# Three elementwise steps of a cross-attention and feed-forward kernel are issued by GpSimd in place of VectorE

## The chip, the cores and the metric

The program runs on 1 core of one Trainium2 chip. The metric is the device time in microseconds (us) of one execution. The kernel before took 1811.93 us, the median of 3 runs (1809.35 to 1813.45).

A core has engines that run their own instruction streams in order and meet at semaphores: TensorE (PE; its weight loads are PEld), VectorE (DVE), ScalarE (ACT), GpSimd (POOL), and SyncE (SP), which here only waits and issues transfers.

## The reference

All inputs are float32. There are 4 batches, with 1024 rows of `x` and 2048 rows of context each, 512 columns, 16 heads of 32.

```python
x = x + xattn(layernorm(x), ctx, ctx, mask, W_q, W_k, W_v, W_o)
x = x + ffn(layernorm(x), rhs)

# xattn
q, k, v = (Q @ W_q.T), (K @ W_k.T), (V @ W_v.T)          # split into 16 heads of 32
scores = einsum('bhqd,bhkd->bhqk', q, k) / sqrt(32)
e = where(mask, exp(clip(scores, -50, 50)), 0)
attn = e / sum(e, -1)                                    # 1 where the sum is <= 0
out = einsum('bhqk,bhkd->bhqd', attn, v) @ W_o.T

# ffn: int8 product with a scale per row of lhs and per column of rhs
q_lhs = clip(round(lhs / lhs_scale), -127, 127)          # lhs_scale = max|row| / 127
y = (q_lhs @ q_rhs) * lhs_scale * rhs_scale
```

## The kernel before

**Segments.** The work is a list of 21 segments. A segment can hold up to three kinds of work: *a*, the projections K, V and Q of a batch; *b*, the attention of a group of 4 heads (32 steps: 2 halves of 512 queries, each over 16 key tiles of 128); *c*, the row tiles (128 rows each) of the batch before: output projection, layer norm, int8 quantisation, feed-forward, residual, store. The first 4 segments have only *a*. The 12 that follow have *a* and *b*, the last 8 of them *c* too, with 2 row tiles each; they run from about 141 to 1375 us, and this text calls them the shared segments. Then come 4 final segments with *b* and 3 row tiles each, to about 1770 us, and the last 4 row tiles by themselves. The remaining entry of the list holds no attention.

**Slots.** A segment has 32 slots, one for each attention step. The tables `BOTH`, `ENDING` and `ENDING_LAST` say at which slot a piece of *a* or *c* is issued (`("F", 0)` is the feed-forward product of row tile 0). Each engine walks over the slots and issues its share; what it does then waits on semaphores with constant values, so the tables set the order on each engine and not the time.

**Attention of a step.** PE writes the scores of 4 heads into 4 banks, ACT turns them into exponentials (`probs`, L1169), PE multiplies these with V (`wsum`, L943). For the denominators DVE adds the exponentials of steps 0 to 13 of a half into `acc` (L1455, 128 x 2048, both operands in SBUF). `probs` is a ring of 4 steps: ACT may write step s only once DVE has added step s - 4.

**End of a half.** Each half that is done goes through a chain, in the slots of the half that follows (`first` is 0 or 16 there): ACT copies `denoms` and `sums` out; SP spreads the denominators (slot first + 2), DVE inverts them (L1463), SP stores the reciprocals and loads them back, broadcast to all rows, into `denoms` (L724, slot first + 5). Then three steps follow: `sums` times `denoms` (L1471, on DVE, behind slots first + 8 and first + 9), the rounded part cast by ACT into `o_hi` (L1271, at first + 10), and `sums` minus that part (L1474, on DVE, behind first + 12 and first + 13). SP then writes both parts to DRAM (`o_parts`, L731, at slot first + 14). These are what the output projection of the next batch reads.

**Row tile.** PE computes the output projection (`O`), DVE adds the residual and takes the row statistics (L1350 to L1354), POOL raises the variance to the power -0.5 (`rstd`, L1545; in the final segments L547, of 128 x 1 elements each). DVE then normalises (L1388, or L1492 in the final segments), finds the maximum, quantises (L1393, L509); ACT rounds (L1191, L521); PE transposes (`T`) and multiplies (`F`); DVE scales the product (L1438, L514) and adds the residual (L1511; in the final segments `add_rows`, L552). SP stores the rows and loads the rows of the next tile into the same buffer, both after `y_added`.

**POOL** has little else to do. At the start of a segment it reads the flag that says whether clipping can be left out (it can, for these inputs) and then releases all `probs_ready` waits of the segment at once.

## Time and profile before

| | |
|---|---|
| median of 3 runs | 1811.93 us |
| profiled execution | 1813.45 us |
| its span in the trace | 1811.6 us |
| PE busy | 1726.3 us (95%), 10808 matmuls |
| DVE busy | 1382.8 us (76%), 1663 instructions |
| ACT busy | 1299.1 us (72%), 1713 instructions |
| POOL busy | 110.7 us (6%), 76 instructions |
| granted PE clock, mean | 0.983 |
| moved by DMA | 295.94 MB, mean 163 GB/s |

The span is the time from the first to the last instruction in the trace; the execution's own time is 1.85 us longer. Busy time of PE is modelled from pipelined matmuls, so a PE that is busy all the time can still be held up inside a matmul stream. The page's 40 slices of the span show PE at 9 tenths or more in nearly all slices, except the first and some of the last ten:

```profile
PE   7999999999999999999999999999998989898986
DVE  5647777777778878787887878788785888787785
POOL 0000000000001010100101010000100000000001
```

### The profile page before, as it was taken

What the parts mean: (1) busy time and instruction counts of PE and PEld (TensorE: products, weight loads), DVE (VectorE), ACT (ScalarE), POOL (GpSimd) and SP (SyncE); (2) the same over time, 40 slices, a digit from 0 to 9 for tenths busy, and PEclk for the clock granted to TensorE, in tenths of its full rate; (3) what the DMA queues carried; (4) which work ended last, traced back from release to release, by engine and by line L of the source; (5) the groups of instructions that cost most, each with busy time, mean ns of one, the idle gap of its engine ahead of it and who ended that gap; (6) DMA issues with size and microseconds to landing.
All of it is one profiled execution on the core that took longest, in us unless ns stands there. A gap on an engine that the chain in (4) does not pass through costs nothing.

```text
span 1811.6 us, 30523 instructions
## 1 busy us (share of the span) xinstructions
PE 1726.3 (95%) x10808; PEld 1015.2 (56%) x10808; DVE 1382.8 (76%) x1663; ACT 1299.1 (72%) x1713; POOL 110.7 (6%) x76
## 2 busy tenths in 40 slices
PE   7999999999999999999999999999998989898986
PEld 6895655555565565656655565666554343343433
DVE  5647777777778878787887878788785888787785
ACT  4557777778777777777777777777775767666672
POOL 0000000000001010100101010000100000000001
PEclk9999999999999999999999999999999999999997
DMA  7686655556665665567566556757557786768632
GB/s 254 212 245 152 159 143 139 141 140 156 158 172 143 166 163 148 169 154 198 125 159 177 147 168 150 198 127 177 157 151 188 196 188 162 162 163 203 157 94 76
DMA packets 231173, 295.94 MB, mean 163 GB/s; under 512 B 28136, under 2 KB 134632, under 8 KB 230504
## 3 DMA queue, kind: packets, MB, share of 16 engines
q1 hardware_dynamic: 228856, 289.21, 61.1%
q10 hardware_dynamic: 2160, 4.72, 0.9%
q8 instruction: 88, 1.44, 0.4%
q14 instruction: 69, 0.57, 0.1%
HBM read 201.59 MB, written 92.00 MB: 162 GB/s over the span
## 4 chain that ended last, share of the span: by engine, by line
PE 78%; issue 8%; DVE 6%; ACT 4%; DMA 2%; POOL 1%; SPq 1%; POOLq 0%; DVEq 0%; ACTq 0%
PE tile L905 24%; PE wsum L943 22%; PE scores L927 21%; ACT probs L1169 3%; PE tile L975 3%; PE scores L905 3%; DVE acc L1455 2%; PE tile L969 2%; PE scores L1073 1%; POOL kmax L547 1%; PE tile L1036 1%; PE tile L1073 1%; DMA v_parts<-v_stage 1%; PE tile L1013 1%; DMA wq_lo<-o_parts 1%
## 5 line engine op out<-in xcount | busy, mean ns | idle before, releaser
L1169 ACT ACTIVATE probs<-scores 128x1024 f32<-128x1024 f32 x939 | 914.1, 1027 | 232.1 <-PE scores L927 177.8
L1455 DVE TENSOR_TENSOR acc<-acc,probs 128x2048 f32<-128x2048 f32 x384 | 878.8, 2288 | 132.4 <-ACT probs L1169 122.3
L943 PE MATMUL wsum<-probs,v_sb 128*32 128x512 f32 x4096 | 501.9, 608 | 0.0
L927 PE MATMUL scores<-q_stack,k_stack 128*128 128x512 f32 x1536 | 444.5, 410 | 9.4 <-ACT probs L1169 8.9
L927 PEld LDWEIGHTS scores<-q_stack,k_stack 128*128 128x128 f32 x1536 | 265.5, 188 | 222.9 <-ACT probs L1169 111.2
L943 PEld LDWEIGHTS wsum<-probs,v_sb 128*32 128x32 f32 x4096 | 111.6, 110 | 257.1 <-issue 230.9
L1545 POOL TENSOR_TENSOR rstd<-var_eps,minus_half 128x1 f32<-128x1 f32 x48 | 79.6, 1658 | 1255.9 <-DVE var_eps L1354 1255.9
L1073 PE MATMUL scores<-q_stack,k_stack 128*128 128x512 f32 x342 | 109.8, 423 | 23.2 <-ACT probs L1169 23.2
L1406 DVE TENSOR_TENSOR squares<-squares 128x128 bf16<-128x128 bf16 x160 | 35.4, 221 | 122.2 <-ACT squares L1209 122.2
L905 PE MATMUL tile<-ctx_hi,wk_hi 128*128 128x256 f32 x412 | 115.6, 281 | 1.8 <-DVE ctx_lo L1364 1.8
L1169 ACT ACTIVATE probs<-tile 128x1024 f32<-128x1024 f32 x85 | 87.5, 1029 | 38.7 <-PE tile L1073 38.6
L905 PE MATMUL tile<-ctx_hi,wk_lo 128*128 128x256 f32 x412 | 115.2, 280 | 0.0
L905 PE MATMUL tile<-ctx_lo,wk_hi 128*128 128x256 f32 x412 | 115.1, 279 | 0.0
L1455 DVE TENSOR_TENSOR acc<-probs 128x2048 f32<-128x2048 f32 x32 | 73.4, 2293 | 48.3 <-ACT probs L1169 47.1
L1073 PEld LDWEIGHTS scores<-q_stack,k_stack 128*128 128x128 f32 x342 | 57.8, 189 | 86.6 <-ACT probs L1169 48.4
L905 PE MATMUL tile<-wv_lo,ctx_hi 128*128 128x512 f32 x208 | 84.2, 405 | 0.0
L905 PE MATMUL tile<-wv_hi,ctx_hi 128*128 128x512 f32 x208 | 83.9, 403 | 0.0
L905 PE MATMUL tile<-wv_hi,ctx_lo 128*128 128x512 f32 x208 | 82.6, 397 | 0.0
L905 PEld LDWEIGHTS tile<-ctx_hi,wk_hi 128*128 128x128 f32 x412 | 77.4, 188 | 5.8 <-issue 2.6
L905 PEld LDWEIGHTS tile<-ctx_hi,wk_lo 128*128 128x128 f32 x412 | 77.4, 188 | 3.1
L905 PEld LDWEIGHTS tile<-ctx_lo,wk_hi 128*128 128x128 f32 x412 | 77.4, 188 | 0.0
L1206 ACT CAST stage_hi<-tile 128x256 fp32r<-128x256 f32 x144 | 53.8, 374 | 29.6 <-PE tile L905 17.1
(235 smaller groups left out, 2041.9 us busy)
## 6 DMA issues: line engine op xcount, KB each, us to landing
k_stack<-k_parts SPq DMA_DIRECT2D x312, 256.0 KB, 7.1
q_stack<-q_parts SPq DMA_DIRECT2D x124, 256.0 KB, 6.8
v_sb<-v_parts SPq DMA_DIRECT2D x80, 256.0 KB, 6.1
v_parts<-v_stage SPq DMA_DIRECT2D x64, 256.0 KB, 5.1
raw<-ctxT SPq DMA_DIRECT2D x27, 512.0 KB, 6.6
k_parts<-stage_hi SPq DMA_DIRECT2D x96, 128.0 KB, 3.5
k_parts<-stage_lo SPq DMA_DIRECT2D x96, 128.0 KB, 2.0
x_in<-x SPq DMA_DIRECT2D x33, 256.0 KB, 3.8
```

Of the source, the lines that this page charges most:

```text
L547: nc.gpsimd.tensor_tensor(one(f_rstd, n), one(f_var, n), minus_half[:, :], ALU.pow).then_inc(fs["rstd_ready"], 1)
L905: last = nc.tensor.matmul(dst, s(kc), m(kc), start=(n == 0), stop=(n == len(todo) - 1))
L927: last = nc.tensor.matmul(scores[:, h, :], k_stack[:, kt // 4, h, (kt % 4) * P:(kt % 4 + 1) * P], q_stack[:, qb, h, :], start=True, stop=True)
L943: last = nc.tensor.matmul(wsum[DH * h:DH * h + DH, :], v_sb[:, kt, DH * h:DH * h + DH], probs[:, n % RING, h, :], start=(kt == 0), stop=(k ...
L969: last = nc.tensor.matmul(dsum[DH * h:DH * h + DH, :], ones[:, :], acc[:, h, :], start=not opened, stop=False)
L975: last = nc.tensor.matmul(dsum[DH * h:DH * h + DH, :], ones[:, :], probs[:, m % RING, h, :], start=False, stop=(m == n + 1))
L1073: last = nc.tensor.matmul(score_banks(seg, n, pair)[:, h, :], k_stack[:, kt // 4, 2 * pair + h, (kt % 4) * P:(kt % 4 + 1) * P], q_stack[:, ...
L1169: nc.scalar.activation(probs[:, slot % RING, 2 * pair:2 * pair + 2, :], score_banks(seg, slot, pair), ACT.Exp, scale=1.0 / math.sqrt(DH)). ...
L1206: nc.scalar.copy(to, src[:, 0:ROWS]).then_inc(sems["hi_done"], 1)
L1406: nc.vector.tensor_tensor(run if opens else both[:, 0:P], both[:, 0:P], both[:, P:2 * P], ALU.max) \
L1455: nc.vector.tensor_tensor(acc[:, :, :], other, probs[:, slot % RING, :, :], ALU.add).then_inc(sems["add_done"], 1)
L1545: nc.gpsimd.tensor_tensor(rstd[:, u:u + 1], var_eps[:, u:u + 1], minus_half[:, :], ALU.pow).then_inc(sems["rstd_ready"], 1)
```

## The change

Three steps are issued by GpSimd (`nc.gpsimd.tensor_tensor`) where VectorE issued them: the product of `sums` and `denoms`, the subtraction that leaves the low part, and the addition of the residual to the feed-forward product. In the segments with attention the product stands at slot first + 6 of POOL's stream, the subtraction at first + 11, the addition at the slot of its `F` piece (in the final segments at the odd slot of the pair of `F`). SP waits for the low part, and stores both parts, at slot first + 13, one slot earlier than before; within a slot this comes ahead of all else that SP does.

```diff
-        def add_rows(eng, tensor_tensor, n):
-
-            eng.wait_ge(fs["y_scaled"], n + 1)
-            tensor_tensor(f_n(n), f_n(n), f_x1(n), ALU.add).then_inc(fs["y_added"], 1)
+        def add_rows(pool, n):
+
+            pool.wait_ge(fs["y_scaled"], n + 1)
+            nc.gpsimd.tensor_tensor(f_n(n), f_n(n), f_x1(n), ALU.add).then_inc(fs["y_added"], 1)
...
-                    if slot == first + 14:
+                    if slot == first + 13:
                         ct.wait_alone(sp, "attn_split", k)
...
-                def normalise(even):
-
-                    for first, k, on in ((0, 0, seg.prev and seg.b), (KT, 1, seg.b)):
-                        if on and even == first + 8:
-                            ct.wait(dve, "recips_loaded", 16 * k)
-                            ct.wait(dve, "sums_copied", k)
-                            nc.vector.tensor_tensor(sums[:, :], sums[:, :], denoms[:, :], ALU.mult).then_inc(sems["attn_normed"], 1)
-                        if on and even == first + 12:
-                            ct.wait(dve, "attn_hi", k)
-                            nc.vector.tensor_tensor(sums[:, :], sums[:, :], o_hi.bitcast(F32), ALU.subtract).then_inc(sems["attn_split"], 1)
...
-                        n = row_tile(seg, pair, "F")
-                        if n is not None:
-                            add_rows(dve, nc.vector.tensor_tensor, n)
                         invert(even)
-                        normalise(even)
...
-                                    if p[0] == "F" and not soon:
-                                        ct.wait(dve, "y_scaled", p[1] + 1)
-                                        nc.vector.tensor_tensor(normed[:, :], normed[:, :], xr[:, :], ALU.add).then_inc(sems["y_added"], 1)
...
+            def normalise(ct, k):
+
+                ct.wait(pool, "recips_loaded", 16 * k)
+                ct.wait(pool, "sums_copied", k)
+                nc.gpsimd.tensor_tensor(sums[:, :], sums[:, :], denoms[:, :], ALU.mult).then_inc(sems["attn_normed"], 1)
+
+            def normalised_lo(ct, k):
+
+                ct.wait(pool, "attn_hi", k)
+                nc.gpsimd.tensor_tensor(sums[:, :], sums[:, :], o_hi.bitcast(F32), ALU.subtract).then_inc(sems["attn_split"], 1)
...
+                        if p[0] == "F":
+                            ct.wait(pool, "y_scaled", p[1] + 1)
+                            nc.gpsimd.tensor_tensor(normed[:, :], normed[:, :], xr[:, :], ALU.add).then_inc(sems["y_added"], 1)
...
+                        n = row_tile(seg, slot // 2, "F")
+                        if n is not None:
+                            add_rows(pool, n)
+                    for first, k, on in ((0, 0, seg.prev), (KT, 1, seg.b)):
+                        if on and seg.b and slot == first + 6:
+                            normalise(ct, k)
+                        if on and seg.b and slot == first + 11:
+                            normalised_lo(ct, k)
```

On DVE, in a shared segment with row tiles, the stream before is this from the quantisation of the first row tile on:

```order
L1388 TENSOR_SCALAR normed<-xr,mean_var,rstd 128x512
L1389 TENSOR_REDUCE amax<-normed 128x1
L1390 TENSOR_SCALAR row_scale<-amax 128x1
L1391 RECIPROCAL inv_scale<-row_scale 128x1
L1393 TENSOR_SCALAR normed<-normed,inv_scale 128x512
L1455 TENSOR_TENSOR acc<-acc,probs 128x2048
L1406 TENSOR_TENSOR kmax<-squares 128x128
L1410 TENSOR_TENSOR stage_lo<-tile,stage_hi 128x256
L1455 TENSOR_TENSOR acc<-acc,probs 128x2048 x3
L1471 TENSOR_TENSOR sums<-sums,denoms 128x512
```

The product stood behind four accumulations. It and the two other steps are gone from this stream. On POOL the same kind of segment (without clipping) is now this, with lines of the changed kernel (L1537 the power, L1521 the product, L1550 the addition, L1526 the subtraction):

```order
L1537 TENSOR_TENSOR rstd<-var_eps,minus_half 128x1 x2
L1521 TENSOR_TENSOR sums<-sums,denoms 128x512
L1550 TENSOR_TENSOR normed<-normed,xr 128x512
L1526 TENSOR_TENSOR sums<-sums,denoms 128x512
L1537 TENSOR_TENSOR rstd<-var_eps,minus_half 128x1 x2
L1521 TENSOR_TENSOR sums<-sums,denoms 128x512
L1550 TENSOR_TENSOR normed<-normed,xr 128x512
L1526 TENSOR_TENSOR sums<-sums,denoms 128x512
```

Before, POOL had only the four power operations there. The product now stands directly behind the power of the first row tile. On SP, at the end of the last shared segment and the start of the final ones, the stream before is:

```order
L667 DMA k_stack<-k_parts 32x4x512 x4
L697 DMA v_sb<-v_parts 128x512
L868 DMA q_parts<-stage_hi 128x256
L868 DMA q_parts<-stage_lo 128x256
L731 DMA o_parts<-denoms 128x512
L731 DMA o_parts<-sums 128x512
L812 DMA safe_row<-safe 1x16x1
L873 DMA v_parts<-v_stage 128x4x128
L558 DMA xr<-x 128x512
L569 DMA wq_hi<-o_parts 128x4x512
L569 DMA wq_lo<-o_parts 128x4x512
```

and with the change:

```order
L731 DMA o_parts<-denoms 128x512
L731 DMA o_parts<-sums 128x512
L667 DMA k_stack<-k_parts 32x4x512 x4
L697 DMA v_sb<-v_parts 128x512
L868 DMA q_parts<-stage_hi 128x256
L868 DMA q_parts<-stage_lo 128x256
L812 DMA safe_row<-safe 1x16x1
L873 DMA v_parts<-v_stage 128x4x128
L558 DMA xr<-x 128x512
L569 DMA wq_hi<-o_parts 128x4x512
L569 DMA wq_lo<-o_parts 128x4x512
```

The two `o_parts` stores moved ahead of a key load (4 transfers), a value load and two query stores; the loads `wq_hi` and `wq_lo`, which read them, stayed where they were.

## Rows read from the trace of the kernel before

**Rows 1.** Busy time by stretch; columns: us, engine busy (x instructions), granted clock, DMA.

```profile
541.00:961.00 420.00, 419.11 (x2694) 252.02 (x2688) 339.84 (x404) 321.35 (x424) 31.26 (x16) 1.00 0.61 161
...
1370.00:1790.00 420.00, 370.68 (x2093) 169.89 (x2092) 319.42 (x291) 273.25 (x314) 23.88 (x14) 0.96 0.67 166
```

**Rows 2.** Waits from 541 to 1370; waiter <- releaser: total us, times, longest.

```profile
DVE acc L1455 <- ACT probs L1169: 68.4, 79, 3.0
...
PE tile L905 <- DVE ctx_lo L1364: 0.9, 1, 0.9
```

**Rows 3.** Timeline, the first row tile of one segment.

```profile
660.72 0.53 SPq L724 DMA_DIRECT2D denoms<-recip_row  x1
...
663.07 2.57 POOL L1545 TENSOR_TENSOR rstd<-var_eps,minus_half 128x1 f32<-128x1 f32 x1 [1.58 <-DVE var_eps L1354]
...
665.68 0.55 DVE L1375 TENSOR_SCALAR x_in<-x_in,mean_var,rstd 128x512 f32<-128x512 f32 x1 [0.44 <-POOL rstd L1545]
...
666.14 0.54 DVE L1388 TENSOR_SCALAR normed<-xr,mean_var,rstd 128x512 f32<-128x512 f32 x1
...
668.35 0.63 ACT L1191 ACTIVATE q<-normed 128x512 bf16<-128x512 f32 x1 [1.22 <-DVE normed L1393]
...
668.88 1.92 ACT L1169 ACTIVATE probs<-scores 128x1024 f32<-128x1024 f32 x2
...
670.52 1.17 PE L927 MATMUL scores<-q_stack,k_stack 128*128 128x512 f32 x4
```

**Rows 4.** Timeline, first row tile of a final segment.

```profile
1501.36 2.57 POOL L547 TENSOR_TENSOR kmax<-kmax,minus_half 128x1 f32<-128x1 f32 x1 [35.02 <-DVE kmax L502]
...
1503.97 0.55 DVE L1492 TENSOR_SCALAR v_stage<-x_in,kmax 128x512 f32<-128x512 f32 x1 [0.44 <-POOL kmax L547]
...
1505.66 0.49 DVE L509 TENSOR_SCALAR v_stage<-v_stage,kmax 128x512 f32<-128x512 f32 x1
...
1506.18 0.63 ACT L521 ACTIVATE raw<-v_stage 128x512 bf16<-128x512 f32 x1 [2.83 <-DVE v_stage L509]
...
1507.77 0.74 PE L1073 MATMUL tile<-q_stack,k_stack 128*128 128x512 f32 x2 [2.93 <-ACT probs L1169]
```

**Rows 5.** Timeline, from the last shared segment into the final ones.

```profile
1361.91 0.62 ACT L1271 CAST denoms<-sums 128x512 fp32r<-128x512 f32 x1
...
1367.89 0.32 SPq L868 DMA_DIRECT2D q_parts<-stage_lo  x1
...
1372.27 0.38 SPq L731 DMA_DIRECT2D o_parts<-denoms  x1
...
1391.79 0.79 PE L905 MATMUL tile<-wo_hi,wq_hi 128*128 128x512 f32 x1 [6.72 <-DMA wq_lo<-o_parts]
```

**Rows 6.** The chain that ended last, same stretch; columns: start us, us, what.

```profile
1372.69 7.17 DMA o_parts<-sums
...
1381.58 10.17 DMA wq_lo<-o_parts
```

**Rows 7.** Line views, moved operations and power; duration in ns min/median/max.

```profile
L1471 DVE TENSOR_TENSOR sums<-sums,denoms x31: 682/685/689, 217.4 to 1758.6; 128x512 f32<-128x512 f32 x31
...
L1511 DVE TENSOR_TENSOR normed<-normed,xr x16: 683/685/690, 578.7 to 1358.2; 128x512 f32<-128x512 f32 x16
...
L552 POOL TENSOR_TENSOR probs<-probs,acc x4: 1259/1261/1262, 1795.3 to 1808.0; 128x512 f32<-128x512 f32 x4
...
L1545 POOL TENSOR_TENSOR rstd<-var_eps,minus_half x48: 547/2573/2632, 23.2 to 1334.7; 128x1 f32<-128x1 f32 x48
```

**Rows 8.** Timeline, one power operation under an accumulation; columns: start us, us, engine, line.

```profile
704.31 2.29 DVE L1455 TENSOR_TENSOR acc<-acc,probs 128x2048 f32<-128x2048 f32 x1
...
704.44 2.57 POOL L1545 TENSOR_TENSOR rstd<-var_eps,minus_half 128x1 f32<-128x1 f32 x1 [10.73 <-DVE var_eps L1354]
...
706.52 0.22 DVE L1406 TENSOR_TENSOR squares<-squares 128x128 bf16<-128x128 bf16 x1
```

**Rows 9.** Busy time by stretch, 1378 to 1381: the DMA share is the last but one.

```profile
1378.00:1381.00 3.00, 3.00 (x29) 0.94 (x32) 0.16 (x1) 2.18 (x4) 0.00 (x0) 1.00 0.33 106
```

More of the change, by code:

```diff
@@ L658, in last_rows_gpsimd @@
                 if n >= FULL + 2:
-                    add_rows(pool, nc.gpsimd.tensor_tensor, n - 2)
+                    add_rows(pool, n - 2)
         def load_k(eng, j, quarter):
@@ L1518, in body @@
                     invert(even)
-                    normalise(even)
                 assert links == ct.per("dve_chain", seg), links
```

## The prediction

> **What bounds the kernel now.** I read the busy time by stretch first, since a mean over the span mixes stages. In the shared segments PE is the bound: of the 420 us from 541 on it is busy 419.11, at a granted clock of 1.00 (the upper of its two levels, 2.4 GHz), with DVE busy 339.84 and POOL 31.26 [rows 1]. In the final segments it is not: 370.68 of 420 us, at a mean clock of 0.96. Second, the waits. From 541 to 1370 us PE waited once, 0.9 us, for anything; DVE waited 68.4 us in 79 places for exponentials, so it catches up with ACT again and again, and work taken from it turns into more waiting there [rows 2]. Third, the timelines of the two places where PE hangs on ACT and ACT on DVE: the first row tile of a shared segment [rows 3] and that of a final segment [rows 4]. Last, the chain of waits into the final segments, the largest single stop: PE stood 6.72 us for `wq_lo`, which SP could load only after the `o_parts` stores had landed [rows 5, 6].
>
> **What leaves DVE.** 31 products and as many subtractions at 0.685 us, 28 additions (16, and 12 in the final segments) at 0.685: 90 x 0.685 = 61.7 us of DVE time [rows 7]; the subtraction and the 12 additions have the same form. I count it as nothing. In the shared segments PE covers it. In the final segments the stop of row tiles 1 and 3 of a segment begins at an accumulation that waited for ACT, and the moved steps stand behind it in DVE's stream, not in it. Lower bound: a saving of 0; a larger one would need a wait of PE that ends on a moved step, and I found none.
>
> **What comes to POOL.** The same 90 instructions at 1.26 us, from the four that POOL ran at the end: 113 us [rows 7]. POOL is idle there; by itself this costs nothing. What matters is what a POOL instruction does to DVE. The rows show one direction. A power of 128 x 1 elements takes 0.55 us at its shortest [rows 7], but the one that began at 704.44, 0.13 us after an accumulation, took 2.57: it ended at 707.01, 0.41 behind the end of the accumulation at 706.60 [rows 8]. So POOL stood still while DVE read two SBUF operands. It did not also wait for `squares`, which DVE had begun at 706.52 with two SBUF operands of its own: POOL got in at the boundary of two DVE instructions. A power holds nothing for long; a product of 512 columns would. I take it that DVE's next instruction of that sort then waits for POOL. The trace has no such pair, so the hold is bounded by 0 and by POOL's whole 1.26 us; I take 1.1, the 1.26 less the 0.14 that the power spent before it touched data (0.55 - 0.41).
>
> The Trainium skill says the same in general: in SBUF — State Buffer, section Who interferes with whom, a DVE instruction with two SBUF inputs, or one in a two-port mode, and a GpSimd instruction that reads SBUF exclude each other for a whole instruction, and the one that issues first keeps the other out. The trace agrees for the accumulation (2.57 us against 0.55); no row shows GpSimd as the winner. By that rule the shared stop would be at its upper bound, 7.7, and the sum +5.1. Perfetto Trace Analysis, section Optimizing Scalar/DVE Operations, warns for the same reason that moving work between these two might not help.
>
> **Where a hold reaches PE: shared segments.** In POOL's new order the product stands directly behind the power of row tile 0. Its reciprocals were requested at 660.72, some 5 us before that power ended at 665.64 [rows 3]. So the product starts then, at the moment when the same power lets DVE go: L1375 from 665.68, L1388 from 666.14. Both read one tensor of 512 columns in 0.54 us, faster than the 0.685 of a two-operand step, so I take them to use both operand paths. L1375 comes first; POOL enters at its end; L1388 and all behind it up to L1393 slip by 1.1, of which some 0.05 is lost in gaps. ACT was already waiting for L1393 (1.22 us before L1191), and its next exponentials follow at once: two in 1.92 us from 668.88, so the second ends at 670.80. PE begins the next scores at 670.52 and needs the first pair then, the second half a microsecond later. Slack: 0.7 for the first (ended at 669.90), about 0.3 for the second. Slip 1.05 less 0.35 is 0.7 us of PE, in a stage that PE bounds. 8 segments have such a tile: 8 x 0.7 = 5.6 us. Bounds: 0 and 8 x (1.26 - 0.3) = 7.7.
>
> **Final segments.** At row tile 1 the product also follows the power (ends at 1503.93), against L1492 from 1503.97 to 1504.52. If POOL enters at its end it is done near 1505.6, before L509 at 1505.66; only the tiny steps between are in its way. I take 0.3 us, bounds 0 and 1.26, in a stop that PE feels in full (2.93 us) [rows 4]. 4 segments: 1.2 us, bounds 0 and 5.0. Row tile 3 has no POOL work near it.
>
> **The other holds.** The three remaining POOL steps of each half of a segment fall among accumulations. Each takes 0.6 us of stream off DVE and may put 1.1 on; in between DVE waits for ACT in most steps [rows 2], and ACT's ring lets an accumulation be late by some steps. Count: 0. What is cut off if this cover is gone is the exponential four steps on.
>
> **SP's order.** At the end of the last shared segment SP stored at 1372.27 and, by the chain, 1372.69; that store took 7.17 us to land, SP waited until 1379.86, and `wq_lo`, issued at 1381.58, took 10.17 [rows 5, 6]. The high part was ready early (ACT's cast at 1361.91), so POOL has the low part by about 1366, and SP can store behind its query store of 1367.89: 4.0 us earlier. The key and value loads that go behind it are due many steps later. The loads of `wq` then start up to 4 us earlier, but the queued transfers have to drain first. From 1378 to 1381 the DMA engines were busy for a share of 0.33 only, so 2.0 of those 3 us stood empty while SP waited [rows 9]. Bounds: these 2.0, which the loads can fill at the least, and 6.72, PE's whole wait. I take 3.8, near the 4.0 by which the store moves. In other segments the store moves too, and PE does not wait for it. SP now waits for the low part ahead of the load of the next `xr`; that may put it 1 to 3 us later, and DVE's later gaps take that up.
>
> **Sum.** -3.8 + 5.6 + 1.2 = +3.0 us, on an execution of 1813.45 (span 1811.6): 1816.5. That execution lay 1.5 above the median; against the median, 1811.93 + 3.0 = 1814.9. That is 0.17%. What a measurement of this kernel can tell from no change is about 0.2%, 3.6 us.
>
> **Rivals.**
> - *No hold on DVE* (chance 0.26). DVE keeps its pace whatever POOL does; only SP's order is left: -2.0 to -6.7, with 3.8 to 5 likeliest, so 1807 to 1810. For it: `squares` kept its 0.22 beside a POOL operation. Against: that operation had one column. This is the case on the faster side; it decides from a hold below 0.3 us at L1388.
> - *POOL wins each meeting* (0.19). The product enters ahead of L1375 and L1492, which were 0.03 to 0.04 us behind the power's end. Then the final stops grow by 1.1 each, 4.4 in all, and the shared ones by 0.96: 7.7. Sum -3.8 + 4.4 + 7.7 = +8.3, so 1820. For it: POOL needs no semaphore to go on. Against: POOL spends 0.14 us before it reads.
> - *The loads drain no sooner* or the terms cancel (0.13): SP's gain is 2.0 and the holds are half of mine (3.4): +1.4, so 1813.
> - The change does what it says for sure; the streams show it.
>
> **Numbers.** The forecast has 0.42, from +0.5 to +5.5 us. It lies half within 3.6 us (0.21) and half above it (0.21). The first rival is faster by more than 3.6 in 0.18, within it in 0.08; the second is slower, 0.19; the third is within, 0.13. So faster 0.18, within 0.42, slower 0.40. The range, with 2 in 10 left out: 1807 to 1821. The forecast's own is 1812.4 to 1817.4.
>
> **What would show it.** In the new trace: the product (L1521) starting at the end of the power and lasting over 1.26 us; L1388 or L1375 starting about 1 us late; ACT's wait before L1191 near 2.3 us in the eight segments, and eight waits of PE for ACT of about 0.7 between 541 and 1370, where there were none; the accumulations lengthened by up to 1.1 us beside POOL; L1492 unchanged; PE's wait for `wq_lo` down to about 3 us. Wrong would be the hold, if DVE's durations stay at 2.29 and 0.54; wrong would be SP's term, if that wait stays at 6.7.

## The result, and the profile after

| | before | after |
|---|---|---|
| median | 1810.86 us (4 runs, 1809.35 to 1813.45) | 1824.25 us (4 runs, 1822.37 to 1825.56) |
| ratio | | 1.0072, 95% interval 1.0054 to 1.0089 |
| profiled execution, span | 1813.45, 1811.6 | 1824.0, 1821.9 |

The change costs 13.4 us. The forecast was 1814.9 us, with a range that ended at 1821.0, so it was wrong. I went through the new trace in the order of the prediction. First the stretches of [rows 1] (us, then PE, PEld, DVE, ACT, POOL busy, clock, DMA share, GB/s):

```profile
541.00:961.00 420.00, 418.56 (x2688) 251.90 (x2692) 342.62 (x380) 321.33 (x424) 83.49 (x40) 1.00 0.62 160
1370.00:1790.00 420.00, 367.76 (x2046) 167.26 (x2058) 315.40 (x249) 271.11 (x312) 87.14 (x40) 0.95 0.68 166
```

PE is busy for 0.55 us less in the shared segments: they lost next to nothing. DVE, which gave 24 instructions away there, is busy for 342.62 us where it was 339.84, so what it does takes longer. The accumulations say by how much (ns min/median/max; before, their longest was 2296):

```profile
L1455 DVE TENSOR_TENSOR acc<-acc,probs x384: 2226/2293/3392, 145.3 to 1775.7; 128x2048 f32<-128x2048 f32 x192
...
L1526 POOL TENSOR_TENSOR sums<-sums,denoms 128x512 f32<-128x512 f32 x31 | 82.1, 2648 | 116.4 <-ACT denoms L1271 116.4
```

The longest accumulation grew by 1.10 us, which is the hold that the forecast took; all together grew by 43.6 us (922.4 against 878.8). The second line is from the page: the subtraction on POOL takes 2.65 us beside them, not 1.26. The waits of PE over the whole span (total, times, longest):

```profile
PE scores L1073 <- ACT probs L1169: 24.8, 43, 3.9
...
PE tile L905 <- DVE v_stage L514: 9.2, 2, 5.9
...
PE tile L905 <- DMA wq_lo<-o_parts: 3.2, 1, 3.2
```

The wait for `wq_lo` fell from 6.72 to 3.25 us. What grew is the wait for `v_stage`, which DVE writes at L514: it was 2.1 us once, and is 9.2 in two, 5.87 and 3.36. PE reached the first output projection at 1387.40, 4.39 us earlier than in [rows 5]; at the feed-forward stop of row tile 1 in the second final segment it was 4.71 us later (1512.48 against 1507.77 in [rows 4]). That is 9.10 us between the two places. 8.58 of it went in the first final segment: from its stop at row tile 1 to its stop at row tile 3 it takes 67.58 us (1406.96 to 1474.54), where it took 59.00. 0.94 is the longer stop at the end (3.87 us, 2.93 before); some 0.4 was gained ahead of 1407. In the first final segment, on SP, and then on ACT, POOL, DVE and PE:

```profile
1411.55 0.34 SPq L697 DMA_DIRECT2D v_sb<-v_parts  x1
1425.70 0.34 SPq L731 DMA_DIRECT2D o_parts<-denoms  x1
...
1426.62 1.87 SPq L667 DMA_DIRECT2D k_stack<-k_parts  x4
...
1430.10 2.98 SPq L569 DMA_DIRECT2D wv_lo<-o_parts  x1
...
1434.94 3.22 SPq L674 DMA_DIRECT2D q_stack<-q_parts  x4
1438.28 0.55 SPq L718 DMA_DIRECT2D den_c<-denoms  x1
```

```profile
1415.74 0.64 ACT L1271 CAST denoms<-sums 128x512 fp32r<-128x512 f32 x1
1419.05 3.27 POOL L552 TENSOR_TENSOR normed<-normed,xr 128x512 f32<-128x512 f32 x1 [12.59 <-DVE normed L514]
1422.27 3.34 POOL L1526 TENSOR_TENSOR sums<-sums,denoms 128x512 f32<-128x512 f32 x1
...
1437.89 4.72 DVE L1455 TENSOR_TENSOR acc<-acc,probs 128x2048 f32<-128x2048 f32 x2 [2.81 <-ACT probs L1169]
1450.26 0.25 DVE L1463 RECIPROCAL recip_c<-den_c 128x16 f32<-128x16 f32 x1 [7.65 <-DMA den_c<-denoms]
1450.43 2.23 DVE L1455 TENSOR_TENSOR acc<-acc,probs 128x2048 f32<-128x2048 f32 x1
1452.57 0.75 DVE L514 SCALAR_TENSOR_TENSOR v_stage<-tile,kmax,rhs_scale 128x512 f32<-128x512 f32 x1
...
1453.47 0.76 PE L905 MATMUL tile<-wo_hi,wq_hi 128*128 128x512 f32 x1 [5.87 <-DVE v_stage L514]
```

In the kernel before, the load of `den_c` and the inversion that reads it were:

```profile
1438.99 0.55 SPq L718 DMA_DIRECT2D den_c<-denoms  x1
...
1448.78 0.25 DVE L1463 RECIPROCAL recip_c<-den_c 128x16 f32<-128x16 f32 x1 [1.43 <-DMA den_c<-denoms]
```

Read the lines from the end. PE waits for L514. L514 stands in DVE's stream behind the inversion L1463, which waits 7.65 us for `den_c` (1.43 us before the change). DVE had come to this point 4.74 us earlier than before, but the load of `den_c` was issued only 0.71 us earlier, and it took 11.96 us to land where it had taken 9.8: it landed 1.5 us later than before. Most of the wait is thus the gain of the hand-over, given back. The load was late because SP issued nothing from 1411.9 to 1425.7: it stood at the store of `o_parts`, for POOL's subtraction. Before, it stood there too (10.6 us, from 1420.6 to 1431.2), but with the four loads of `k_stack` issued ahead of the stand. Now they stood behind it, and when SP went on they ran together with `wv`, `y`, `xr` and `q_stack`. The low part itself was late on POOL: ACT had cast the high part by 1416.38, but in POOL's stream the addition L552 stands ahead of the subtraction and waited for L514, and both then took over 3.2 us beside accumulations, until 1425.61. The granted clock, by windows (us, PE busy, clock, DMA share, GB/s):

```profile
1447.00:1453.40 6.40, 0.60 (x2) 0.89 0.98 215
1453.40:1458.70 5.30, 5.23 (x12) 0.50 0.29 74
```

While PE stood, the clock fell to 0.50, the lower of its two levels, and the twelve matmuls of the output projection took 5.3 us; before, at clock 1.00, they took 2.9. So the stop cost 5.87 us and 2.4 more behind it. The same happens once more in the third final segment, where before the change DVE waited 3.88 us and PE 2.10:

```profile
1649.69 0.25 DVE L1463 RECIPROCAL recip_c<-den_c 128x16 f32<-128x16 f32 x1 [5.13 <-DMA den_c<-denoms]
...
1652.90 0.47 PE L905 MATMUL tile<-wo_hi,wq_hi 128*128 128x512 f32 x1 [3.36 <-DVE v_stage L514]
```

Two more places of the forecast. The first row tile of a shared segment, which answers to [rows 3]:

```profile
661.81 2.57 POOL L1537 TENSOR_TENSOR rstd<-var_eps,minus_half 128x1 f32<-128x1 f32 x1 [1.58 <-DVE var_eps L1354]
...
664.42 0.55 DVE L1375 TENSOR_SCALAR x_in<-x_in,mean_var,rstd 128x512 f32<-128x512 f32 x1 [0.44 <-POOL rstd L1537]
664.88 0.54 DVE L1388 TENSOR_SCALAR normed<-xr,mean_var,rstd 128x512 f32<-128x512 f32 x1
665.13 1.44 POOL L1521 TENSOR_TENSOR sums<-sums,denoms 128x512 f32<-128x512 f32 x1 [0.74 <-DMA denoms<-recip_row]
665.46 0.69 DVE L1389 TENSOR_REDUCE amax<-normed 128x1 f32<-128x512 f32 x1
```

The product did not start at the end of the power: it waited 0.74 us for its reciprocals, L1388 had begun 0.25 us before it, and nothing on DVE was held. In seven of the eight segments the product began 0.19 to 0.38 us behind L1388, in one later still; L1388 never took longer than 0.54 us, and L1393 was held once, by 0.27 us. ACT's waits for L1393 were 7.8 us in eight, where they had been 8.3. And row tile 1 of a final segment, which answers to [rows 4]:

```profile
1505.12 2.57 POOL L547 TENSOR_TENSOR kmax<-kmax,minus_half 128x1 f32<-128x1 f32 x1 [20.38 <-DVE kmax L502]
...
1507.66 1.27 POOL L1521 TENSOR_TENSOR sums<-sums,denoms 128x512 f32<-128x512 f32 x1
1507.73 1.50 DVE L1481 TENSOR_SCALAR v_stage<-x_in,kmax 128x512 f32<-128x512 f32 x1 [0.44 <-POOL kmax L547]
...
1512.48 0.73 PE L1073 MATMUL tile<-q_stack,k_stack 128*128 128x512 f32 x2 [3.87 <-ACT probs L1169]
```

Here the reciprocals were there. POOL's product began 0.07 us ahead of the normalisation, which then took 1.50 us where it took 0.55, and PE stopped for 3.87 us and not 2.93. The third final segment has the same meeting. In the fourth the product came later and held the quantisation L509 (1.28 us against 0.49); PE stopped for 3.73 us. In the first it began 0.16 us behind L509, and PE's stop stayed at 2.93.

### The profile page after: what moved, and what is told of

Its sections match the earlier page's. It is cut to its first block, busy times and chain, and to the rows that moved or that the text cites. A ratio compares the mean times of both kernels' runs of the same rounds, so it can differ in the third digit from the quotient of the medians.

```text
span 1821.9 us, 30494 instructions
## 1 busy us (share of the span) xinstructions
PE 1728.2 (95%) x10779; PEld 1016.9 (56%) x10808; DVE 1389.8 (76%) x1573; ACT 1298.4 (71%) x1713; POOL 314.3 (17%) x166
## 4 chain that ended last, share of the span: by engine, by line
PE 75%; issue 8%; DVE 5%; ACT 4%; DMA 3%; POOL 2%; SPq 2%; ACTq 0%; POOLq 0%; DVEq 0%
PE tile L905 23%; PE wsum L943 21%; PE scores L927 21%; ACT probs L1169 3%; PE tile L975 2%; PE scores L905 2%; DVE acc L1455 2%; PE tile L969 1%; DMA den_c<-denoms 1%; POOL kmax L547 1%; PE scores L1073 1%; DMA v_parts<-v_stage 1%; POOL sums L1526 1%; PE tile L1036 1%; PE tile L1073 1%
## 5 line engine op out<-in xcount | busy, mean ns | idle before, releaser
L1455 DVE TENSOR_TENSOR acc<-acc,probs 128x2048 f32<-128x2048 f32 x384 | 922.4, 2402 | 131.9 <-ACT probs L1169 114.4
L1537 POOL TENSOR_TENSOR rstd<-var_eps,minus_half 128x1 f32<-128x1 f32 x48 | 79.6, 1659 | 699.1 <-DVE var_eps L1354 699.1
L1526 POOL TENSOR_TENSOR sums<-sums,denoms 128x512 f32<-128x512 f32 x31 | 82.1, 2648 | 116.4 <-ACT denoms L1271 116.4
L1521 POOL TENSOR_TENSOR sums<-sums,denoms 128x512 f32<-128x512 f32 x31 | 54.3, 1753 | 228.3 <-DMA denoms<-recip_row 228.3
```

The lines of the kernel that those rows point to most:

```text
L1455: nc.vector.tensor_tensor(acc[:, :, :], other, probs[:, slot % RING, :, :], ALU.add).then_inc(sems["add_done"], 1)
L1521: nc.gpsimd.tensor_tensor(sums[:, :], sums[:, :], denoms[:, :], ALU.mult).then_inc(sems["attn_normed"], 1)
L1526: nc.gpsimd.tensor_tensor(sums[:, :], sums[:, :], o_hi.bitcast(F32), ALU.subtract).then_inc(sems["attn_split"], 1)
L1537: nc.gpsimd.tensor_tensor(rstd[:, u:u + 1], var_eps[:, u:u + 1], minus_half[:, :], ALU.pow).then_inc(sems["rstd_ready"], 1)
```

## Experiments

Ratios are to the kernel before, which ran between the others on the same chip. "Mixed segments" in the expectations are the shared ones. The kernels by their parts (*late*: the subtraction on DVE behind slot first + 12, as before; *early*: behind first + 10, see below):

| label | steps, shared / final | store's slot, shared / final | median us | ratio (95%) |
|---|---|---|---|---|
| before | DVE late / DVE late | 14 / 14 | 1809.98 to 1811.43, by chip | 1 |
| after | POOL / POOL | 13 / 13 | 1824.25 | 1.0072 (1.0054-1.0089) |
| store14 | POOL / POOL | 14 / 14 | 1813.52 | 1.0023 (1.0012-1.0034) |
| store13_mixed_pool | POOL / POOL | 13 / 14 | 1810.24 | 1.0000 (0.9988-1.0013) |
| mixed_pool_store14 | POOL / DVE late | 14 / 14 | 1812.75 | 1.0015 (1.0002-1.0027) |
| final_on_dve | POOL / DVE late | 13 / 13 | 1824.19 | 1.0073 (1.0061-1.0085) |
| store13 | DVE late / DVE late | 13 / 13 | 1865.55 | 1.0311 (1.0293-1.0329) |
| store13_not_final | DVE late / DVE late | 13 / 14 | 1855.87 | 1.0247 (1.0233-1.0261) |
| early_lo_store14 | DVE early / DVE early | 14 / 14 | 1808.74 | 0.9985 (0.9976-0.9995) |
| early_lo_store13 | DVE early / DVE early | 13 / 14 | 1805.10 | 0.9969 (0.9958-0.9981) |
| early_lo_store13_again | the same | 13 / 14 | 1806.49 | 0.9973 (0.9963-0.9984) |
| early_lo_store13_all | DVE early / DVE early | 13 / 13 | 1810.16 | 0.9990 (0.9978-1.0003) |
| final_store_behind_loads | POOL / POOL | 13 / 13, behind `k_stack` | 1812.07 | 1.0011 (0.9998-1.0023) |
| den_c_before_q | POOL / POOL, `den_c` loaded earlier | 13 / 13 | 1815.07 | 1.0023 (1.0011-1.0034) |
| early_lo_add_pool | DVE early, only the additions on POOL | 13 / 14 | 1806.99 | 0.9976 (0.9965-0.9987) |
| mixed_pool_only | POOL / DVE early | 13 / 14 | 1808.10 | 0.9980 (0.9970-0.9990) |
| final_pool_only | DVE early / POOL | 13 / 14 | 1810.32 | 0.9989 (0.9977-1.0002) |

The kernels were measured in groups on several chips, so times of different groups are compared by their ratios. Most ratios are uncertain by about 0.0012, and a difference of two by 3 to 4 us.

**Which part costs: the store's slot or the engine.** Two theories after the first look. A: the store's place in SP's order costs in the final segments. B: the holds of DVE cost.

```diff
# store14 = after, with
-                    if slot == first + 13:
+                    if slot == first + 14:
# store13 = before with first + 13; store13_not_final:
+                    if slot == first + (14 if seg.final else 13):
```

> The changed kernel with SP's store back at its old slot, the three steps on GpSimd. Theory A: PE's wait for wq_lo is 6.7 again (+4.4), the new wait of 5.87 for v_stage with the low clock behind it (8.6 us in all between 1407 and 1474) is gone, and only the longer stops of the later final segments stay (+3 to +6): 1814 to 1820 us. Theory B: the 8.6 us are lost here as well, 1828 us.

Measured 1813.52, ratio 1.0023, just below theory A's range and far from B's 1828. By the ratios the slot is worth 1.0072 - 1.0023, or 8.9 us of the 13.0 that 1.0072 stands for. PE waits 0.5 us for `v_stage` in its trace. The wait for `wq_lo` is 4.17 us and not 6.7, since POOL has the low part earlier even with the old slot.

> The kernel before with one line of the change alone: SP's store of the attention's parts one slot earlier, the three steps still on VectorE. Theory A (the store's place in SP's order costs in the final segments: SP stands at the store until the low part is subtracted, four loads of k_stack wait behind it, and the load of den_c behind those lands no earlier than before): the wait for wq_lo at the hand-over falls from 6.72 to about 3, and most of it is lost again in the first final segment, 1808 to 1814 us. Theory B (the loss comes from GpSimd's steps that hold VectorE's accumulations): nothing is on GpSimd here, so all of the gain stays, 1806.5 us (1810.9 less 4.4), and no wait of PE over 3.6 us follows 1407.

> The kernel before with the store one slot earlier in the mixed segments only, in its old slot in the final ones. Theory A: the gain of 4.4 at the hand-over is kept if den_c of the first final segment lands earlier with it, 1806.5 us; if its load lands at 1448.8 as before, VectorE waits 1.43 + 4.4 = 5.8 us for it and the gain is given back, 1810 to 1812. Theory B: 1806.5 us as well.

Measured 1865.55 and 1855.87. Both theories missed this by 40 us and more. With the low part made late on DVE, the store one slot earlier costs most in the shared segments. Before the change SP waited 186.5 us in all for the low part; in store13 (total, times, longest) it waited 413.3:

```profile
SPq L302 <- DVE sums L1474: 413.3, 31, 23.7
```

And PE, from 541 to 1370 us, has a wait that it did not have before:

```profile
PE scores L927 <- ACT probs L1169: 15.8, 11, 3.0
```

In these 829 us PE does 5107 matmuls where it did 5318, 4% less, which is some 33 us of its work; the waits shown are 15.8 us of that, and the rest is not traced. Behind the store stand the stores of `stage_hi` and `stage_lo`, whose buffers ACT and DVE wait to write, and the loads of `xr` and `x_in` (in store13_not_final DVE waits 44.3 us for `xr` in 8 places, 18.2 in the changed kernel). Which of them costs how much is not shown. In the changed kernel POOL has the low part sooner (it starts at 578.47 in one segment, DVE did at 585.46), and SP waited 251.5 us in all.

```diff
# final_on_dve = after, with POOL's three steps under "if not seg.final"
# and DVE's old add_rows and normalise inside "if seg.final"
```

> The changed kernel with the three steps back on VectorE in the final segments alone (GpSimd does them in the mixed ones; the store stays in its new slot). Theory A: the same as the kernel before with only the store moved, 1808 to 1814 us. Theory B: the whole loss lies in the final segments' steps on GpSimd, 1806.5 us. If the shared segments cost after all (+5.6 was forecast), it is 1812 by theory B.

Measured 1824.19, as slow as the change itself. Both ranges missed. The run changes two things at once. The stops of row tile 1 are 2.75 to 2.94 us again, except for one of 4.22. But the low part is late on DVE, and SP stands 138.6 us for it in eight places of the final segments, where the change has 100.2. Its trace has the wait for `den_c` at 9.51 us and PE's for `v_stage` up to 7.7. So the chain over `den_c` does not need POOL's steps, which is theory A's mechanism; what these steps cost, the run does not tell.

**In which segments does the slot cost?**

> The changed kernel with the store in its new slot in the mixed segments and in its old one in the final segments. The store's slot has cost 10.7 us (1824.2 against 1813.5). Theory A (the loss is in the final segments: there the store stands ahead of four loads of k_stack in the same slot, they run together with the loads of wv, and den_c lands late): 1812 to 1814 us, DVE's wait for den_c at about 1450 is back to 1 to 3 us. Theory B (it is the mixed segments' late loads of xr and x_in): 1822 to 1825 us.

Measured 1810.24, ratio 1.0000: a little below theory A's range, and theory B is out. The slot costs (1.0072 - 1.0000) x 1811 = 13.0 us in the final segments, and gains (1.0023 - 1.0000) x 1811 = 4.2 us in the shared ones with the hand-over. In its trace the four loads of `k_stack` go out during what was SP's stand, and `den_c` is issued 3.7 us sooner and lands in time:

```profile
1414.51 1.73 SPq L667 DMA_DIRECT2D k_stack<-k_parts  x4
1425.96 0.34 SPq L731 DMA_DIRECT2D o_parts<-denoms  x1
...
1434.60 0.55 SPq L718 DMA_DIRECT2D den_c<-denoms  x1
...
1443.51 0.25 DVE L1463 RECIPROCAL recip_c<-den_c 128x16 f32<-128x16 f32 x1 [0.56 <-DMA den_c<-denoms]
```

PE has no stop for `v_stage` here. From the stop of row tile 1 to that of row tile 3 the first final segment takes 58.85 us (67.58 with the change) and the third 58.55 (63.97). These two differences, 8.7 and 5.4 us, make 14.1, about what the slot costs by the runs; both stretches hold a stop for `v_stage` of the changed kernel.

**Is it the four loads, and is it `den_c`?** Two edits of the changed kernel that leave the store in slot 13.

```diff
# final_store_behind_loads: in the final segments, behind load_k of the same slot
+                    if step == 13:
+                        chain(seg, ct, slot, store=False)   # only the store
# den_c_before_q: one slot earlier, ahead of load_q
-                    if slot == first + 2:
+                    if slot == first + (1 if seg.final else 2):
```

> The changed kernel; in the final segments the store stays in its new slot but goes behind the four loads of k_stack that this slot issues (it stood ahead of them). The store's slot in the final segments has cost 0.72% (ratio 1.0072 against 1.0000 with the old slot there). Theory A (the loads that stand behind the store cost it, by running later together with the others and pushing den_c's load): 1810 to 1813 us, VectorE's wait for den_c at about 1450 falls from 7.65 to under 2 us. Theory B (SP's standing costs, whatever stands behind it in that slot): 1820 us or more.

Measured 1812.07, ratio 1.0011 (0.9998 to 1.0023), in theory A's range. This is less of a new test than it looks: in the final segments nothing stands between these four loads and the old slot 14, so SP's order is that of store13_mixed_pool, built another way. What the two runs show together is that the slot's whole effect in the final segments is the order of the store and the four loads, two neighbours, and that it is worth 11 us by one and 13 by the other. SP still stands 9.0 us there. The profiled execution (1817.45 us) is the longest of its twelve; in its trace the wait for `den_c` at that place is gone:

```profile
1448.63 0.25 DVE L1465 RECIPROCAL recip_c<-den_c 128x16 f32<-128x16 f32 x1
```

> The changed kernel with the load of den_c one slot earlier in the final segments, ahead of the four loads of q_stack: SP issues it at about 1434.9 and not 1438.3, its data are there at 1434.2. Theory A (VectorE waits for den_c, and PE behind it for v_stage): the wait of 7.65 falls by 3 to 6 us, PE's wait of 5.87 with it and part of the low clock after it: 1816 to 1820 us. Theory B (den_c's wait is not what PE waits for): 1824 us.

Measured 1815.07, ratio 1.0023 (1.0011 to 1.0034), somewhat better than expected: 8.9 us come back by moving one 8 KB load. DVE's wait fell from 7.65 to 1.77 us, and PE's 5.87 is not in its trace:

```profile
1449.33 0.26 DVE L1463 RECIPROCAL recip_c<-den_c 128x16 f32<-128x16 f32 x1 [1.77 <-DMA den_c<-denoms]
...
1452.54 0.47 PE L905 MATMUL tile<-wo_hi,wq_hi 128*128 128x512 f32 x1
```

The stops of row tile 3 that follow are longer, 5.11 and 4.79 us in two segments where the change has 3.44 and 3.58, which takes part of the gain. So the chain from SP's stand over the late loads and `den_c` to L514 and PE is shown at both ends.

**Is it the standing?** If SP's stand costs, an earlier low part should make the store's slot cheap, on either engine. On DVE the subtraction can go two slots earlier, since ACT's cast is long done by then:

```diff
# early_lo_store14 = before, with
-                        if on and even == first + 12:
+                        if on and even == first + 10:
# early_lo_store13: also slot == first + (14 if seg.final else 13)
# early_lo_store13_all: also slot == first + 13
```

> The kernel before with the low part's subtraction two slots earlier on VectorE and nothing else. Its store is still last in its slot, so SP issues it no sooner than the old slot lets it, but does not stand for it. Theory A: at the hand-over the store goes out some 2 us sooner as on GpSimd (PE's wait for wq_lo about 4.2 instead of 6.72): 1807 to 1809 us. Theory B (nothing but the slot matters): 1810.0 us.

> The kernel before, all steps on VectorE, with the low part's subtraction two slots earlier (behind ACT's cast, which ends at 575.6 while the subtraction starts at 585.5) and the store one slot earlier in the mixed segments. Theory A (a store moved up costs what SP stands there until its data is there; with the subtraction at slot 12 that was 17 us in a half and 46 us in all): SP hardly stands, the 46 us are gone, and the hand-over's gain stays, 1806 to 1809 us. Theory B (the place ahead of the loads of xr and x_in costs by itself): 1820 us or more.

> All steps on VectorE, the low part's subtraction two slots earlier, the store in slot 13 in the final segments too. With the store in slot 14 there the ratio was 0.9969. In the changed kernel SP stood some 13 us at the store of the first final segment; here the low part is there about 4 us sooner (1421.5 against 1425.6), so SP stands about 7. Theory A (what is lost grows with the time that SP stands): 1807 to 1813 us. Theory B (only the order counts, by any standing): 1818 us.

Measured 1808.74, 1805.10 and 1810.16 (ratios 0.9985, 0.9969 and 0.9990), in or just below theory A's ranges. The loss of store13_not_final is gone with the subtraction moved, 0.9969 against 1.0247: 50 us, and SP's wait for the low part is 203.7 us in all, not 383.2. A store in slot 13 of the final segments still costs 0.21%, 3.8 us (uncertain by 3), against 13.0 us in the changed kernel. That the loss grows with SP's stand is not shown by this: SP stands 11.5 us at the first of these stores in early_lo_store13_all, not the 7 expected, and 13.8 in the changed kernel. What differs more is PE's wait for `v_stage`, 2.50 us once, against 5.87 and 3.36. In the trace of early_lo_store13 the low part is done at 1421.55, and:

```profile
1413.90 1.73 SPq L667 DMA_DIRECT2D k_stack<-k_parts  x4
...
1420.87 0.68 DVE L1474 TENSOR_TENSOR sums<-sums,denoms 128x512 f32<-128x512 f32 x1
1421.64 0.34 SPq L731 DMA_DIRECT2D o_parts<-denoms  x1
```

`early_lo_store13` is the kernel that beats both: 0.31% faster than before, and 1.0% faster than the change, with no step on POOL. Run again beside two of the next kernels it had 1806.49 us and 0.9973 (0.9963 to 0.9984).

**The holds, measured by segment.** At the same store slots the kernel with all three steps on POOL is 0.31% slower than the one with all on DVE, early (1.0000 against 0.9969), 5.6 us. With the store in its old slot it is 6.9 us (1.0023 against 0.9985). Which segments?

> The three steps on GpSimd in the mixed segments, on VectorE in the final ones, the store in its old slot everywhere. The three steps on GpSimd in all segments have cost 3.5 us (1813.5 against 1810.0) with this slot. Theory A (that cost is the holds of VectorE in the final segments, where the row tiles stop PE; the mixed segments only bring the low part 4 us sooner): 1806 to 1809 us. Theory B (it comes from the mixed segments): 1813.5 us.

> The best kernel so far (subtraction two slots earlier on VectorE, store in slot 13 in the mixed segments and 14 in the final ones, 1805.1 us) with the 28 additions of the row tiles on GpSimd. It is 5.6 us faster than the same slots with all three steps on GpSimd (1810.2, ratios 0.9969 and 1.0000). Theory A (each step on GpSimd costs by holding VectorE's two-operand work in the final segments, the additions as much as the others): 1806 to 1808 us. Theory B (the additions are off the path and free VectorE): 1803 to 1805 us.

> The three steps on GpSimd in the mixed segments at the changed kernel's slots; in the final segments all on VectorE with the subtraction two slots earlier; the store in slot 13 in the mixed and 14 in the final segments. It differs from early_lo_store13 (ratio 0.9969) by the engine of the steps in the mixed segments alone. The forecast's term (+5.6: GpSimd's product holds VectorE behind the power of row tile 0, in eight mixed segments): 1810 to 1812 us. Rival (the product does not meet a two-operand instruction of VectorE there, and the held accumulations are not waited for): 1804 to 1806 us.

> The same comparison for the final segments: there the three steps on GpSimd at the changed kernel's slots, in the mixed ones on VectorE with the early subtraction, the store in slots 13 and 14. Theory A (GpSimd's steps hold the chain of row tile 1 by 0.9 us at three or four of PE's stops, and the low part is 3 to 4 us later): 1807 to 1810 us. Theory B (the forecast's +1.2 or less): 1805 to 1806.5 us.

> early_lo_store13 once more beside these two, as their common measure: 1803 to 1807 us, ratio 0.996 to 0.998 by its first runs.

`mixed_pool_store14` came to 1.0015, not to be told from store14's 1.0023: theory A's range for it, 1806 to 1809, failed. It compares with a late subtraction in the final segments, so it could not settle the size. `early_lo_add_pool` (the 28 additions on POOL) came to 1806.99, 0.9976 (0.9965 to 0.9987), within the uncertainty of 0.9969, so it does not decide between its theories. The last three ran together: 1808.10 (0.9980, 0.9970 to 0.9990) with POOL in the shared segments alone, 1810.32 (0.9989, 0.9977 to 1.0002) with POOL in the final ones alone, 1806.49 with none. The first lies between the forecast's range and the rival's, the second just above theory A's. So the shared segments' steps on POOL cost 1.6 us (1.3 by the ratios), which cannot be told from 0, and the final segments' 3.8 us (2.9 by the ratios), at the edge of what can be told. The trace of `final_pool_only` (1819.0 us, the longest of its twelve executions, which reach from 1804.84) shows three of the four stops of row tile 1 lengthened, to 3.35, 3.88 and 3.88 us, and a later stop of 4.97 us that was 3.53 before the change:

```profile
1606.77 0.87 PE L1073 MATMUL scores<-q_stack,k_stack 128*128 128x512 f32 x2 [3.88 <-ACT probs L1169]
1667.80 1.22 PE L1073 MATMUL scores<-q_stack,k_stack 128*128 128x512 f32 x2 [4.97 <-ACT probs L1169]
```

Whether the product holds DVE at this stop differs from trace to trace: three of four stops are longer in the changed kernel and here, two in store13_mixed_pool (3.87 and 4.03 us), and in store14 they are 2.93, 2.93, 2.93 and 3.14.

## Why the prediction was wrong, point by point

- **SP's order: the step that failed.** It priced the store's move at the hand-over, -3.8 us, and said "In other segments the store moves too, and PE does not wait for it." The price was right: -4.39 us in the trace, with the low part's earlier time in it (store14 has that alone: PE waited 4.17 us and began at 1389.51). By the runs the slot alone is worth -4.2 us in the shared segments, uncertain by 3. The sentence on the other segments asked only who waits for the *store*, and put the final segments at nothing. It did not ask what stands behind it while SP waits for the low part: there four key loads of the same slot, and behind them the load of `den_c`. PE did not wait for the key loads, as the prediction says ("due many steps later"), but for `v_stage` over `den_c`. That was worth +13.0 us (11.0 by the second build), more than any term of the sum. The prediction did name the loads of `xr` behind the store and let DVE's gaps take them up. That held for the changed kernel (DVE waited 18.2 us for `xr` in 8 places, PE for nothing), but only since POOL has the low part early: store13_not_final shows +45 us when it is late.
- **The hold.** Right in its size: taken as 1.1 us from one power operation, measured as 1.10 on the accumulations at most, 0.95 on L1481 and 0.79 on L509.
- **Shared segments, +5.6.** Did not happen; measured 1.6 us at most likely, not to be told from 0. The step that failed is "So the product starts then": it took the reciprocals to be there within 5 us of their request. They were issued at 659.28 in the new trace and the product could start at 665.13, 5.85 us later, when L1375 and L1388 had already begun. A margin of 0.2 to 0.4 us between L1388 and the product decided it in seven of the eight segments.
- **Final segments, +1.2.** Undersized. In two of the four segments the second rival (*POOL wins each meeting*) was right: the product was ahead of the normalisation by 0.07 us and held it for 0.95 us. In a third it held the quantisation by 0.79 us. Three stops of PE are 3.73 to 3.87 us against 2.93, 2.7 us in all; the runs give 3.8 us for these steps, uncertain by 3. L1492 (now L1481) was to stay unchanged and did not.
- **The other holds, 0.** Right: the accumulations grew by 43.6 us, and PE did not wait for it in the shared segments.
- **Leaving DVE is worth nothing.** Right as far as the runs go: at the same slots the kernels with the steps on DVE, early, are the faster ones.
- **The sum.** The steps' total was not far off (+6.8 forecast, 5.6 and 6.9 measured at the two pairs of slots), but by luck: the shared segments' 5.6 was 1.6, the final ones' 1.2 was 3.8. The price of the hand-over was right, and the missing term is +13.0. From the kernel before, the steps at the old slot make +4.2 us (their cost, less what the earlier low part gives), the slot in the shared segments -4.2, the slot in the final ones +13.0. That these add up to 13.0, the ratio 1.0072, is no confirmation, since each is the difference of two neighbouring ratios; what confirms the last is the 14.1 us of the two stretches in the traces. The range held no case for it, because no rival asked what else SP does.

## What to carry to other kernels

When a wait moves up in an in-order queue, write down every instruction that now stands behind it *in each stage of the program*, with the time at which the awaited data come, and not only who waits for the moved transfer; here the order of a store and the loads next to it was worth 11 to 13 us. A transfer's slot is only as early as its data, so first move the producer (here the subtraction by two slots: 50 us between the same store slot with it and without), then the transfer. And a step moved to another engine meets other instructions there: its start is set by the last of its inputs, and here a few tenths of a microsecond decided which side was held.

## What the runs showed of the hardware that I had not expected

- GpSimd's two-input operation on 512 columns takes 1.26 us with nothing beside it and 2.65 us in the mean among DVE's accumulations (L1526), which themselves take up to 3.39 instead of 2.29. In these meetings both sides lose, and 61.7 us taken off DVE left it busier (1389.8 us against 1382.8). The accumulations have 43.6 of the 68.7 us that this makes.
- A DVE operation with one SBUF input of 512 columns was held for the whole of GpSimd's product when it started 0.07 us after it (1.50 us against 0.55), but an equal one that had begun 0.25 us before it was not lengthened (0.54). The Trainium skill (SBUF — State Buffer, section Who interferes with whom) says that the instruction that issues first keeps the other out; both meetings agree, with these numbers. Near 0.1 us the recorded starts no longer tell who is first. In store13_mixed_pool the normalisation was recorded at 1692.59, the product at 1692.68, and it was the normalisation that was held (1.66 us, the product 1.28); in store14 the product, 0.14 us behind (1601.13 and 1601.27), was the one that took longer (1.55, the normalisation 0.55). The kinds of DVE instruction are a point apart: a reduction that began beside the product kept its 0.69 us.
- The clock: 5.87 us in which PE waited brought the granted clock from 1.00 to 0.50 for the twelve matmuls after it, 2.4 us more than at the upper level. One stop so cost 1.4 times its length.
- A stand of the issuing engine empties the DMA engines. Before the change too they stood empty, from 1426 to 1431 us. With the change the stand is longer, and the loads that it held back come all at once behind it. From 1411 to 1448 us of the changed kernel, in 40 slices, the busy tenths of the DMA engines and what they moved:

```profile
DMA  3271000000000000299596989999999999999999
GB/s 91 106 206 44 0 0 9 0 0 0 0 0 0 0 0 0 77 376 221 44 109 122 226 199 208 272 297 281 365 392 390 387 405 383 215 219 235 216 209 216
```

  The load of `den_c`, 8 KB, took 11.96 us behind that traffic; before the change it took 9.8.
